# Eight-headed attention: weights split by tokens and turned by transposing transfers, scores in five banks, outputs two steps behind, first queries projected in the stage before

## The reference

```python
def _L1_xattn_ref(x, context, Wq, Wk, Wv, Wo, bo):
    H, D = 8, 64
    SCALE = D ** (-0.5)
    q = (x @ Wq).reshape(B, Nq, H, D)
    k = (context @ Wk).reshape(B, Nkv, H, D)
    v = (context @ Wv).reshape(B, Nkv, H, D)
    sim = jnp.einsum('bihd,bjhd->bhij', q, k) * SCALE
    attn = jax.nn.softmax(sim, axis=-1)
    out = jnp.einsum('bhij,bjhd->bihd', attn, v).reshape(B, Nq, H * D)
...
```

## Time and profile before

| | us |
|---|---|
| median of three runs | 998.07 |
| lowest, highest | 995.18, 999.36 |
| the profiled execution, timed | 997.65 |
| its span in the trace | 995.9 |
| mean granted TensorE clock (1 is full speed) | 0.946 |

### The profile page before, as it was taken

The page is one execution under the profiler, slowest core; times in us unless marked ns, Lnnn a source line. Parts: engine busy times, 40 slices in busy tenths (PEclk is TensorE's granted clock), DMA queues, the critical chain, the costliest instruction groups (busy, mean ns, idle before and its releaser), DMA issues. The chain is left out here.

```text
span 995.9 us, 23453 instructions
## 1 busy us (share of the span) xinstructions
PE 841.9 (85%) x9338; PEld 553.7 (56%) x9338; DVE 774.9 (78%) x1432; ACT 652.3 (66%) x1182; POOL 374.0 (38%) x372
## 2 busy tenths in 40 slices
PE   1276869798489889999958999997899988999997
PEld 0122223233156645655535776765699975778786
DVE  7899989935668989888767999985878876667443
ACT  4589689888468544543338888885787866656431
POOL 1043444322227322000037888885334822224220
PEclk9978789799769989999999999999999999999999
DMA  5402414050131030000040000000200000000000
GB/s 152 85 2 36 50 28 60 12 75 1 56 115 44 2 122 17 2 1 1 1 173 2 3 3 3 3 3 13 64 2 2 2 2 1 1 11 13 12 22 33
DMA packets 21676, 30.55 MB, mean 31 GB/s; under 512 B 6001, under 2 KB 17983, under 8 KB 20417
## 3 DMA queue, kind: packets, MB, share of 16 engines
q1 hardware_dynamic: 18816, 26.44, 11.4%
q10 hardware_dynamic: 2752, 2.62, 0.9%
HBM read 18.56 MB, written 2.10 MB: 21 GB/s over the span
## 5 line engine op out<-in xcount | busy, mean ns | idle before, releaser
L589 ACT ACTIVATE t_pT<-t_sc 128x1536 f32<-128x1536 f32 x96 | 136.7, 1454 | 29.5 <-PE t_sc L696 29.1
L269 POOL TENSOR_SCALAR_AFFINE_SELECT t_pT<-t_pT 128x512 f32<-128x512 f32 x64 | 73.5, 1169 | 168.2 <-ACT t_pT L589 168.2
L696 PE MATMUL t_sc<-t_qk 32*128 32x512 f16 (+3 forms) x1152 | 86.7, 357 | 48.9 <-DMA t_qk<-t_sin_parts 26.3
L696 PEld LDWEIGHTS t_sc<-t_qk 32*128 32x128 f16 x1152 | 36.7, 99 | 107.8 <-issue 55.1
L717 PE MATMUL t_ot<-t_pT,t_v 128*17 128x512 f32 (+3 forms) x768 | 81.9, 538 | 12.5 <-DVE t_ou L433 5.5
L2766 POOL TENSOR_SCALAR_AFFINE_SELECT r_att<-r_att 128x1024 f16<-128x1024 f16 x64 | 68.7, 1099 | 27.1 <-DVE r_att L2815 27.1
L2268 ACT ACTIVATE m_sg<-m_psg 128x512 f32<-128x512 f32 x32 | 19.1, 596 | 56.7 <-PE m_psg L2311 56.7
L1983 PE MATMUL c_pso<-ck_VO,c_pT 128*128 128x256 f16 x480 | 55.0, 273 | 1.4 <-DVE c_pT L1824 1.4
L1983 PEld LDWEIGHTS c_pso<-ck_VO,c_pT 128*128 128x128 f16 x480 | 46.3, 98 | 6.7 <-DVE c_pT L1824 1.6
L1894 ACT ACTIVATE c_pt<-c_pss,c_mx 128x154 f32<-128x154 f32 x128 | 48.4, 415 | 2.3 <-DVE c_mx L1807 2.3
L2332 PE MATMUL m_acc<-gw_down,m_hp 128*128 128x256 f16 x384 | 47.2, 273 | 3.1 <-DVE m_hp L2224 2.6
(11 more groups left out here) (611 smaller groups left out, 2411.7 us busy)
## 6 DMA issues: line engine op xcount, KB each, us to landing
t_qk<-t_cos_parts SPq DMA_DIRECT2D x24, 128.0 KB, 5.1
t_qk<-t_sin_parts SPq DMA_DIRECT2D x24, 128.0 KB, 6.6
x<-in_x ACTq DMA_DIRECT2D x4, 512.0 KB, 6.0
out_x<-x SPq DMA_DIRECT2D x8, 256.0 KB, 2.1
r_rcos<-in_ret_cos SPq DMA_DIRECT2D x1, 1280.0 KB, 7.9
r_rsin<-in_ret_sin SPq DMA_DIRECT2D x1, 1280.0 KB, 10.4
t_qk<-t_cos_parts SPq DMA_DIRECT2D x16, 64.0 KB, 2.6
gw_raw<-in_gateT SPq DMA_DIRECT2D x1, 1024.0 KB, 7.5
```

Of the source, the lines that this page charges most:

```text
L269: last = g.affine_select(out=blk, in_=blk, compare_op=ALU.is_ge, fill=0.0, base=0, pattern=[[0, 4], [1, P]], channel_multiplier=-1)
L589: a.activation(pT[:, at:at + 3, :].rearrange("p a s -> p (a s)"), sc[s % 2][:], ACT.Exp, scale=CURVE * CURVE / math.sqrt(2 * DH)).then_inc ...
L696: last = t.matmul(sc[s % 2][:, 512 * k + at:512 * k + at + w], qk[r, g % 3, 1, of_k, P * i:P * i + P], qk[r, g % 3, 0, of_q, q0:q0 + w], s ...
```

## The change

**Turning.** For tiles 0 to 14 the weights are no longer transposed on TensorE. ScalarE's `part_high` casts all ten blocks of `pn` to f16 in one instruction (1280 columns), VectorE's `part_low` subtracts in one instruction, both into a new buffer `ph` (two, for even and odd tiles), with tokens still on the partitions. SP then issues one transposing DMA per tile, from `ph` to `pT`. It waits for `part_low` of the tile and for the output of two tiles before, whose `pT` it overwrites; `part_high` waits for the transfer of two tiles before. The last tile, 15, is still turned on TensorE, in banks of the score ring.

**Banks.** The two banks `pst` go to the scores: five banks in a ring, of which each tile takes three, so the next tile's scores need only wait for the exponentials that free their bank.

**Order.** `output` moves from tile s - 2 to tile s - 3, `project` from s + 1 to s + 2, `copy_q` and `x_low` likewise, `add` from s - 3 to s - 4. On VectorE the `maxima` come first in a step, and `signs.scales`, which waits for a load, moves from ahead of everything to the end of step 0.

**First queries.** `project` and `copy_q` become methods of `Opening`. Tiles 0 and 1 are projected in retention's step 17 into retention's banks `psq` and `pss`; their q copies and one exponential, with its table load, stand at the end of retention's list on ScalarE. The low parts of x of tiles 0 and 1 move into the gate of retention's last tile.

```diff
@@ class Opening
+        self.qT = room[:, 1408:2432].rearrange("p (t c k) -> p t c k", t=2, c=4)
+        self.q_ready, self.q_copied = sem("q_ready"), sem("q_copied")
...
+    def project(self, t_, t, keys, psq):
+        if t >= self.FIRST:
+            t_.wait_ge(self.q_copied, t)
+        t_.wait_ge(self.x_split, t + 1)
...
+    def copy_q(self, a, t, psq):
+        a.wait_ge(self.q_ready, t + 1)
+        a.mul(self.qT[:, t % 2].rearrange("p c k -> p (c k)"), psq[:], QSCALE).then_inc(self.q_copied, 1)
@@ headed_attention
-    GROUPS = ((1, 4, 8), (0, 0, 4), (0, 8, 10))
+    RING, LAST = 5, NT - 1
+    GROUPS = ((3, 4, 8), (4, 0, 4), (0, 8, 10))
...
-        pT = sb("pT", [P, 2, 2, SLOTS, P], F16)
+        ph, pT = sb("ph", [P, 2, 2, SLOTS, P], F16), sb("pT", [P, 2, 2, SLOTS, P], F16)
...
+        def bank(t, k):
+            return (3 * t + FIRST.index(k)) % RING
...
         def _(sp):
             signs.load(sp, ins)
+            for t in range(LAST):
+                sp.wait_ge(parted, t + 1)
+                wait(sp, out_ready, t - 1)
+                sp.dma_start(pT[:, t % 2].rearrange("p a s k -> p (a s) k"), ph[:, t % 2].rearrange("p a s k -> p (a s k)"), transpose=True).then_inc(p_landed[t % 2], 16)
...
+            def part_low(t):
+                if inside(t) and t < LAST:
+                    q = t % 2
+                    v.wait_ge(parted_high, t + 1)
+                    v.tensor_tensor(flat(ph[:, q, 1]), flat(pn[:, q]), flat(ph[:, q, 0]), ALU.subtract).then_inc(parted, 1)
...
-            signs.scales(v)
             for s in STEPS:
-                x_low(s + 1)
-                p_low(s - 2, 1)
+                maxima(s, 0)
                 weigh(s - 1)
-                add(s - 3)
-                p_low(s - 2, 2)
-                maxima(s, 0)
                 maxima(s, 1)
-                p_low(s - 1, 0)
                 maxima(s, 2)
-                signs.on_vector(v, s)
+                x_low(s + 2)
+                part_low(s - 1)
+                add(s - 4)
+                for j in range(3):
+                    p_low(s - 1, j)
+                if s == 0:
+                    signs.scales(v)
+                signs.on_vector(v, s - 1)
...
+            def part_high(t):
+                if inside(t) and t < LAST:
+                    q = t % 2
+                    a.wait_ge(main_weighed, t + 1)
+                    a.wait_ge(rest_weighed, t + 1)
+                    wait(a, p_landed[q], 16 * (t // 2))
+                    a.copy(flat(ph[:, q, 0]), flat(pn[:, q])).then_inc(parted_high, 1)
...
             for s in STEPS:
+                exps(s, 0)
                 high_x(s + 2)
-                high_p(s - 2, 2)
-                normalise(s + 4)
-                high_p(s - 1, 0)
-                exps(s, 0)
-                high_p(s - 1, 1)
+                part_high(s - 1)
+                for j in range(3):
+                    high_p(s - 1, j)
                 exps(s, 1)
                 exps(s, 2)
-                copy_q(s + 1)
+                normalise(s + 4)
+                copy_q(s + 2)
...
                     for n, h in enumerate(ORDER):
-                        if n == 0:
-                            wait(t_, exp_done, 3 * t)
+                        k, c0 = next((k, CTX * hs.index(h)) for k, hs in enumerate(BANKS) if h in hs)
+                        if n < 3:
+                            wait(t_, exp_done, 3 * t + FIRST.index(k) - RING + 1)
...
             def output(t):
                 if inside(t):
                     b, q = t // TB, t % 2
-                    t_.wait_ge(p_split, 3 * (t + 1))
+                    if t < LAST:
+                        t_.wait_ge(p_landed[q], 16 * (t // 2 + 1))
+                    else:
+                        t_.wait_ge(p_split, 3)
                     wait(t_, x_done, t)
...
             for s in STEPS:
-                turn_p(s - 1, 0)
-                turn_p(s - 1, 1)
-                project(s + 1)
-                output(s - 2)
-                turn_x(s + 3)
-                turn_p(s - 1, 2)
-                score(s + 1)
+                score(s + 1)
+                project(s + 2)
+                turn_x(s + 3)
+                for j in range(3):
+                    turn_p(s - 1, j)
+                output(s - 3)
@@ retention
                     L(v.tensor_tensor(heads, heads, cen[:, q], ALU.mult))
+                    if t == NT - 1:
+                        opening.low(v, 0, psq)
+                        opening.low(v, 1, pss[:, 0])
...
+                if s == NT + 1:
+                    opening.copy_q(a, 0, psq)
                 z_high(s - 2)
...
+            opening.copy_q(a, 1, pss[:, 0])
+            a.activation(sm[:, 0, 0, 0:1], rowtile[:, 0:1], ACT.Exp)
...
+                if s == NT + 1:
+                    opening.project(t_, 0, keys, psq)
                 turn_z(s - 2)
+                if s == NT + 1:
+                    opening.project(t_, 1, keys, pss[:, 0])
```

More of the change, by code:

```diff
@@ L942, in low @@
         v.tensor_tensor(self.xT[:, t % 2, 2:4, :], ps[:, 0:D].rearrange("p (c k) -> p c k", c=2), self.xT[:, t % 2, 0:2, :], ALU.subtract).then_inc(self.x_split, 1)
+    def project(self, t_, t, keys, psq):
+        if t >= self.FIRST:
+            t_.wait_ge(self.q_copied, t)
+        t_.wait_ge(self.x_split, t + 1)
+        for ec in range(4):
+            for c in range(2):
+                for px, pw in ((0, 0), (0, 1), (1, 0)):
+                    last = t_.matmul(psq[:, P * ec:P * ec + P], keys.wq16[:, pw, c, P * ec:P * ec + P], self.xT[:, t % 2, 2 * px + c, :],
+                                     start=(ec + c + px + pw == 0), stop=(c + px == 2), skip_group_check=True)
+        last.then_inc(self.q_ready, 1)
+    def copy_q(self, a, t, psq):
+        a.wait_ge(self.q_ready, t + 1)
+        a.mul(self.qT[:, t % 2].rearrange("p c k -> p (c k)"), psq[:], QSCALE).then_inc(self.q_copied, 1)
 class Early:
@@ L1747, in headed_attention @@
             sem(n) for n in ("total_ready", "main_weighed", "rest_weighed", "p_turned", "p_high", "p_split"))
+        parted_high, parted, p_landed = sem("parted_high"), sem("parted"), [sem(f"p_landed{q}") for q in range(2)]
         out_ready, x_done = sem("out_ready"), sem("x_done")
@@ L1771, in weigh_rest @@
                     g.wait_ge(total_ready, t + 1)
-                    wait(g, p_turned, 3 * (t - 1))
+                    wait(g, parted, t - 1)
                     rest = pn[:, q, NH:SLOTS, :].rearrange("p g (h k) -> p (g h) k", k=32)[:, :, 0:REST]
@@ L1934, in project @@
             def project(t):
-                if inside(t):
-                    t_.wait_ge(x_split, t + 1)
-                    wait(t_, q_copied, t)
-                    for ec in range(4):
-                        for c in range(2):
-                            for px, pw in three:
-                                last = mm(psq[:, P * ec:P * ec + P], keys.wq16[:, pw, c, P * ec:P * ec + P], xT[:, t % 2, 2 * px + c, :],
-                                          start=(ec + c + px + pw == 0), stop=(c + px == 2), skip_group_check=True)
-                    last.then_inc(q_ready, 1)
+                if inside(t) and t >= opening.FIRST:
+                    opening.project(t_, t, keys, psq)
             def score(t):
@@ L1961, in turn_p @@
             def turn_p(t, j):
-                if inside(t):
-                    bank, a, b = GROUPS[j]
+                if t == LAST:
+                    b, s0, s1 = GROUPS[j]
                     if j == 0:
                         t_.wait_ge(main_weighed, t + 1)
-                        wait(t_, p_split, 3 * (t - 1) + 1 if t else 0)
-                    if j == 1:
-                        wait(t_, p_split, 3 * t)
                     if j == 2:
                         t_.wait_ge(rest_weighed, t + 1)
-                        t_.wait_ge(p_split, 3 * t + 2)
-                    for k in range(a, b):
-                        last = t_.transpose(pst[:, bank, P * (k - a):P * (k - a) + P], pn[:, t % 2, k, :], ident)
+                    for k in range(s0, s1):
+                        last = t_.transpose(pss[:, b, P * (k - s0):P * (k - s0) + P], pn[:, t % 2, k, :], ident)
                     last.then_inc(p_turned, 1)
@@ L2679, in on_tensor, with retention @@
             self.project_first(t_, ps)
-def retention(nc, x, ins, ahead, opening):
+def retention(nc, x, ins, ahead, opening, keys):
     with ExitStack() as ctx:
@@ L2921, in _ @@
                     opening.offsets(v, (s - 9) // 6)
-                if s == NT:
-                    opening.low(v, 0, psq)
-                    opening.low(v, 1, pss[:, 0])
         @block.scalar
@@ L3760, in program @@
                 opening = Opening(known.enter_context(Signals(nc)), x, early.room)
-                retention(nc, x, ins, ahead, opening)
+                retention(nc, x, ins, ahead, opening, keys)
             with ExitStack() as outer:
```

42 lines of the change are left out of this document (19 added, 23 removed).

## The result

In five runs each, the changed kernel took 1005.66 us (1003.87 to 1007.70) and the kernel before 997.81 (995.18 to 999.36): a ratio of 1.008, with a 95% interval from 1.0062 to 1.0099. The forecast was 994.6, with slower by over 0.5% at 0.26; the change is 0.8% slower. That lies inside the forecast's range (987 to 1012), but on the other side of no change than the 994.6. The profiled execution spans 1005.1 us against 995.9, at a mean clock of 0.933 against 0.946.

What follows compares the result with a forecast made beforehand. TensorE's instruction stream was taken as the bound, except at the stage's ends. Stage -3.9, clock +0.7 and retention's end -0.3 sum to -3.5 us on the median 998.07, giving 994.6 us; range 987 to 1012.

Steps and rivals of the forecast that it cites:

- 1.8 us in all: Eight mid-stage steps: extra for outputs waiting for an add behind new statistics and casts, making each step 6.36 us.
- TensorE's step: Mid-stage attention: ten turning matmuls go, 1.24 us a step, so the step falls from 7.37 to 6.13 us.
- Cast: ScalarE: three copies out of PSUM, 1.58 us a tile, become one 1280-column cast of 1.22, at most 1.26 us.
- Transfer: Transposing DMA per tile, 640 KB: 5.5 us taken from issue to the wake-up behind it; harmful over 8.
- Loop: Two pT buffers tie transfer, cast, subtraction, add and output: step is the larger of 6.13 and (D + 6.7)/2, D the transfer time.
- Filling: Start of the stage, paced by VectorE's program: first output at 26.4 us, against 20.6 before.
- the 0.7 for the clock: Lower granted clock in the longer, emptier start of the stage: 1.5 us or 0, taken as 0.7.
- Three steps set by VectorE: Late steps with the rows' low parts and spread on VectorE: 7.7, 7.6 and 8.1 us, 23.4 together.
- Drain: End of the stage: 5.0, 7.7 and 4.0 us, with about 4 us of idle TensorE before output(14).
- End of retention: Projections of tiles 0 and 1 moved there are hidden by TensorE's idle time; z 0.3 us sooner, counted as -0.3.
- rival (b): Slower: transfer too long, deciding point 8.0 us; at 9.5 us, +14.8 us, 1009.4. Chance 0.21.
- Rival (a): Faster: late steps and drain run at TensorE's pace, -6.5 us with no clock loss, 988. Chance 0.32.

Runs made afterwards that it cites:

- the run with writing alone: The changed kernel with each GpSimd mixture replaced by an instruction that only writes zeros (4096 f16 columns): 998.61 us, ratio 1.0009.
- pieces: The changed kernel with all its work, each GpSimd mixture split into four instructions of 512 columns, two a step in steps 10 to 17: 998.97 us, ratio 1.0009.
- the best kernel: The changed kernel with output two steps behind, add ahead of the subtraction and mixtures in 512-column instructions: 981.82 us, ratio 0.9845.

## Why the prediction was wrong

**The step that failed is the price of the new subtraction.** The prediction wrote of cast and subtraction: "These casts read PSUM and the new ones SBUF; I allow 0.2 us either way for each." The subtraction alone took 1.49 us, as forecast, but beside a mixture 4.00. The difference in where it reads, which the sentence names and passes over, was worth 2.5 us four times. The run with the mixtures left out gives back 9.0 us in these four steps, the run with writing alone shows that it is the reading, and pieces give back 8.5 of it there, 6.5 in the whole stage, with all the work kept.

The trace of before had the sign. GpSimd's share of the weights, in the earlier trace rows 1507 ns on average, took 1.57 us beside VectorE's scaling of the weights, which has two SBUF operands and 1.22 us, and 0.53 us the one time it started when that scaling was done (717.90 to 719.13). GpSimd's timeline in the kernel before:

```profile
720.17 0.53 POOL L1774 TENSOR_TENSOR c_pn<-c_pt,c_tot 128x208 f32<-128x208 f32 x1
...
724.61 1.57 POOL L1774 TENSOR_TENSOR c_pn<-c_pt,c_tot 128x208 f32<-128x208 f32 x1 [2.72 <-DVE c_tot L1814]
```

I used the 1.51 as the cost of the work and never asked why 208 columns should take so long. The Trainium skill, page "SBUF — State Buffer", section "Who interferes with whom", states the rule: a VectorE instruction with two SBUF inputs and a GpSimd instruction that reads SBUF exclude each other, and whichever comes second waits until the first is done; one that only writes does not. The traces agree in all three points, with 4.00 us beside a mixture, 1.49 beside a memset, and 1.57 against 0.53 on GpSimd's side. I had not weighed it. The scaling that the added write held up has only one SBUF tensor as its input, so it falls outside this rule.

**The second step that failed is the wait for the add.** I had written that output(t) waits for the add behind the subtraction, and priced it at "1.8 us in all". Placing the add first gave 9.3 us by the medians, 9.4 in the stage, and with the mixtures out of the way 135.1 - 126.7 = 8.4, of which 7.8 from the first output on. I had costed it with each wait at its usual length, but it hands on every lateness of subtraction, cast and landing to TensorE.

**Point by point.** *TensorE's step*: 6.25 us in mid-stage where nothing waits; forecast 6.13 to 6.4, right. *Cast*: 1.26 to 1.32 us; I took 1.22 and gave 1.26 as the bound, slightly low. *Transfer*: ten of 15 landed in 4.8 or 4.9 us, five in 5.3 to 6.7; I took 5.5, right in size, but not one number. *Loop*: its terms add up to 6.6 rather than the 6.7 written; the formula is right in kind; with 6.5 and 6.6 us it gives 6.6 a step, and two of the first six steps were 7.11 and 7.21. *Filling*: first output 27.7 against 26.4. Right before it, from 715.38 with no wait between, scores took 2.42 us and the projection 2.68, at a granted clock of 0.50, where 1.31 and 1.50 are usual: 2.3 us more, so the 0.7 for the clock was too little. The slow first scores (2.33) matter little: in the run with pieces and add first they took 1.34, and the first output came at 27.6. *Three steps set by VectorE*: 23.4 forecast. With both causes gone they take 6.02, 5.24 and 6.42, so that term was 5.7 too large and hid a part of the error: VectorE has room for the rows' low parts. *Drain*: 16.7 forecast, 20.6 measured. The 4 us of idle TensorE before output(14) came as forecast (3.90); what I missed is that the clock falls after such waits, so that two of these outputs took 5.98 and 5.10 us, and a wait of 4.81 before output(12) behind a landing of 6.7 us. *End of retention*: both projections were hidden as forecast, and the 0.3 us came. From the last step of the spread (678.93 before, 679.23 after) to the last add (690.81, 690.82) VectorE's timeline has 11.88 and 11.59 us. This execution had come to that place 0.3 us later, which hides it in the stage's start.

**The sum.** First output +1.3, outputs 0 to 6 -0.4, 6 to 9 +7.3, 9 to 12 +0.9, 12 to 15 +3.9: 12.9 us, from 128.9 to 141.8. The 128.9 is without the clock's 0.7, which the forecast's -3.5 has in it; the spans give +9.2. From the first output on the stage missed by 11.6 us (114.1 against 102.5), while taking both causes away gives 16.8: other terms, the three steps above all, were too long and hid some 5 us of the error.

**The rivals.** Slower was right in sign for a reason I had not named: rival (b) put it on the transfer, which was faster than its deciding point of 8.0 in every tile. The price per transfer was too low as well: for a transfer of 9.5 us I gave 14.8 us more, and doubling the transfer added 28.8 to the kernel after, the clock being again what I had left out. Rival (a), the late steps at TensorE's pace, is what the kernel does once the two causes are away: 989.9, where I had said 988.

**What stays open**: how much the two causes share (1.1 us by the stages, 1.6 from the first output on, 3.4 by the medians, whose executions spread over 4 to 6 us) and how that divides between the clock and the loop; no run kept the clock up. Which kinds of VectorE instruction a GpSimd write holds up was not tried: only the scaling of three columns was caught. And whether the best kernel could lose its 5.2 us of waits for landings with a third buffer was not tried.

## What to carry to other kernels

When an edit changes where an operand is read from, ask which other engine uses that door at that moment. A short GpSimd instruction that takes three times as long in some rows than in others is the sign to look for. An edit that only takes work out for a test can collide too: the write added here cost 2.2 us. Put what TensorE waits for (here the add that frees its only output bank) ahead of anything in the same list that can be late, and give a new transfer the smallest delay in steps that its landing allows, since each step more is paid in the filling and again in the loop of its buffers.

## What the hardware showed that I had not expected

**A transposing transfer of 640 KB from SBUF to SBUF** moves its 2592 packets in most cases in 3.2 us, some 210 to 220 GB/s (one ran at 290, and one in its second half), and lands in ten of 15 cases 4.8 to 4.9 us after its issue. Of the two pages of the Trainium skill that the prediction set beside it, "Advanced Engine Details and Errata", section "X-Bar Transpose (TRN2)", is nearer with 350 to 400 GB/s, but this transfer was slower than that; by the other, "VectorE: DVE Perf Modes", section "The three transpose paths", 20 blocks one after another would be an estimated 26 us, and no transfer here took that. Here are its line's landings and the DMA queues in two windows around single transfers of the kernel after, 763.4 to 768.3 and 730.2 to 736.8 us (packets, MB, share of 16 engines):

```profile
DMA to landing us min/median/max: 4.8/4.9/6.7
```

```profile
q1 hardware_dynamic: 2592, 0.66, 70.0%
```

```profile
q1 hardware_dynamic: 2592, 0.66, 52.2%
q8 instruction: 1, 0.02, 0.9%
```

In the second a packet of the instruction queue falls into the window, and the transfer lands after 6.5 us. All five landings of 5.3 us and more have such a packet beside them (5.3, 6.5, 6.6, 6.0, 6.7), and of the ten of 4.8 or 4.9 only one has. That the packet causes the delay is read from this coincidence; no run moved one.

**The clock is part of most long waits of TensorE.** In the kernel after, outputs that came after waits of 2.10, 2.98, 4.81 and 3.90 us took 5.10, 5.04, 5.98 and 5.10 us, the others 3.44, though one came after 2.84. Beside the waits themselves that is 7.5 us more of TensorE's time in the stage.
